# Pooling of an audio layer: eleven of each sixteen pairs multiplied on GpSimd and five on VectorE, sums two products behind

## The reference, cut to what matters

```python
k = 8                                   # x: (128, 64, 750), padded to 752 steps = 94 windows
xp = x.reshape(B, F, nw, k).transpose(0, 2, 3, 1)
scores = einsum('bwkf,of->bwko', xp, w) + b
weights = softmax(scores, axis=2)       # over the 8 steps of a window
pooled = sum(xp * weights, axis=2)      # (128, 94, 64)
```

## Time and profile before

| what | value |
|---|---|
| median of 3 runs | 1019.79 us (1017.86 to 1020.41) |
| the profiled execution, its own time | 1019.19 us |
| its span, first to last instruction | 1017.5 us |
| first spread matmul of the pooling to its last sum | 34.5 to 141.8 us |
| mean granted TensorE clock | 0.944 |

### The profile page before, as it was taken

How to read it: one execution, slowest core, us unless ns; L and a number is a source line. 1 busy time by engine, 2 the same in 40 slices (tenths; PEclk the granted TensorE clock), 3 DMA queues, 4 the chain that set the end, 5 groups by cost and what they waited for, 6 DMA issues and landing times. The chain is left out here.

```text
span 1017.5 us, 37672 instructions
## 1 busy us (share of the span) xinstructions
PE 898.6 (88%) x15018; PEld 577.8 (57%) x15018; DVE 763.6 (75%) x1287; ACT 423.6 (42%) x710; POOL 488.2 (48%) x551
## 2 busy tenths in 40 slices
PE   3677668998937999999999999999999999799995
PEld 2233245555525666666666666666666666446663
DVE  4588863887983888888788888888888888747773
ACT  2333423112713444444444444444444444257774
POOL 3355631110007666666666666666666666212220
PEclk9777877998977999999999999999999999979998
DMA  8765000324102111111111111111111111001111
GB/s 300 263 223 202 1 0 1 55 54 115 31 0 64 50 49 50 52 52 52 48 45 48 50 52 52 52 49 46 48 49 50 52 52 53 2 3 29 29 29 32
DMA packets 64446, 63.25 MB, mean 62 GB/s; under 512 B 37081, under 2 KB 55068, under 8 KB 64412
## 3 DMA queue, kind: packets, MB, share of 16 engines
q1 hardware_dynamic: 63884, 61.25, 20.4%
q10 hardware_dynamic: 528, 1.54, 0.4%
HBM read 52.93 MB, written 6.75 MB: 59 GB/s over the span
## 5 line engine op out<-in xcount | busy, mean ns | idle before, releaser
L1163 ACT ACTIVATE sq<-ps_dot 128x752 f32<-128x752 f32 x192 | 153.1, 798 | 302.6 <-PE ps_dot L1042 302.6
L1042 PE MATMUL ps_dot<-q_st,k_blk 32*64 32x94 f32 x6144 | 169.4, 247 | 3.1 <-POOL k_blk L1002 3.1
L1042 PEld LDWEIGHTS ps_dot<-q_st,k_blk 32*64 32x64 f32 x6144 | 134.4, 133 | 64.6 <-issue 50.0
L1002 POOL TENSOR_TENSOR k_blk<-k_turn,hmask 128x384 f32<-128x384 f32 x64 | 65.3, 1020 | 177.8 <-ACT k_turn L1151 177.8
L1210 DVE TENSOR_REDUCE sums<-prob 128x94 f32<-128x564 f32 x128 | 148.0, 1201 | 2.0 <-ACT prob L1156 2.0
L1006 POOL TENSOR_TENSOR k_mix<-k_cm,cols 128x768 f32<-128x768 f32 x64 | 119.8, 1872 | 0.0
L988 POOL TENSOR_TENSOR v_blk<-v_rep,vmask 128x384 f32<-128x384 f32 x128 | 106.6, 854 | 6.8 <-PE ps_m L1074 6.8
L1091 PEld LDWEIGHTS ps_a<-q_st,k_mix 64*64 64x64 f32 x3072 | 77.1, 132 | 56.4 <-issue 48.2
L1091 PE MATMUL ps_a<-q_st,k_mix 64*64 64x94 f32 x3072 | 101.0, 250 | 0.8 <-DVE prob L1198 0.8
L1156 ACT ACTIVATE prob<-prob,cols 128x564 f32<-128x564 f32 x128 | 91.1, 758 | 20.4 <-DVE prob L1198 20.4
L1181 DVE TENSOR_REDUCE row_max<-ps_a 128x94 f32<-128x564 f32 x128 | 89.3, 741 | 12.4 <-PE ps_a L1110 12.4
(11 more groups left out here) (225 smaller groups left out, 1389.7 us busy)
## 6 DMA issues: line engine op xcount, KB each, us to landing
v_rep<-v_rows SPq DMA_DIRECT2D x256, 96.0 KB
x_g<-in_x_dram SPq DMA_DIRECT2D x15, 1500.0 KB, 6.7
v_rows<-tok SPq DMA_DIRECT2D x32, 96.0 KB
q_st<-q_cm SPq DMA_DIRECT2D x64, 47.0 KB
out_dram<-rows SPq DMA_DIRECT2D x16, 188.0 KB
x_g<-in_x_dram ACTq DMA_DIRECT2D x1, 1500.0 KB, 7.4
top_rows<-tok SPq DMA_DIRECT2D x16, 32.0 KB
top<-top_rows SPq DMA_DIRECT2D x1, 512.0 KB, 3.4
```

The source lines that it names most:

```text
L1002: return pool.tensor_tensor(k_blk[:, a, :, kind], view.unsqueeze(2).broadcast_to([128, NTAU, 4, 8]), k["hmask4"][:].unsqueeze(1).unsqueeze ...
L1042: mm = pe.matmul(ps_dot[64 * hg:64 * hg + 64, (a + g) % 2, b, col:col + N], k_blk[rows, a, 2 * (2 * g + t2) + mi].rearrange("p k h m -> p ...
L1163: act.activation(sq[:, :, :, 2 * g:2 * g + 2, :].rearrange("p mi b t n -> p b mi (t n)"), ps_dot[:, (a + g) % 2, :, 0:4 * N].rearrange("p ...
```

## The change

GpSimd gets eleven pairs of each group (`SENT`: 1, 2, 4, 5, 7, 8, 10, 11, 13, 14, 15), VectorE five (`OWN`: 0, 3, 6, 9, 12). `w_odd` becomes `w_sent`, and the semaphores `even_*` and `odd_*` become `own_*` and `sent_*`. A sent pair may now lie in either place of `ps_spread`, so TensorE waits for whoever reads the pair two before. `sent(g, a, m)` sums GpSimd's product number m; in a group VectorE calls it up to the product that is two behind, so the last four of a group (7 to 10) are summed in the next group, behind its first own product. ScalarE takes the next scores behind its seventh copy instead of its fifth, GpSimd its two parts of the split behind its eighth and ninth product, and VectorE the two halves of the softmax behind its fourth and fifth own pair.

```diff
+    OWN = tuple(range(0, GP - 1, 3))
+    SENT = tuple(n for n in range(GP) if n not in OWN)
...
+    def buffer_of(a, m):
+        return (a * len(SENT) + m) % 2
...
-                        for products in (s["even_done"], s["odd_done"]):
-
-                            sp.wait_ge(products, (2 * n + a - 2) * (GP // 2) + 2 * q + 2)
+                        sp.wait_ge(s["own_done"], (2 * n + a - 2) * len(OWN) + own_before(4 * q + 4))
+                        sp.wait_ge(s["sent_done"], (2 * n + a - 2) * len(SENT) + sent_before(4 * q + 4))
...
-                    pe.wait_ge(s["odd_out" if n % 2 else "even_done"], g * HP + n // 2)
+                    last = (n - 2) % GP
+                    freed, before, per = ("own_done", own_before, len(OWN)) if last in OWN else ("sent_out", sent_before, len(SENT))
+                    if n >= 2:
+                        pe.wait_ge(s[freed], g * per + before(n - 1))
+                    elif not (isinstance(g, int) and g == 0):
+                        pe.wait_ge(s[freed], (g - 1) * per + before(last + 1))
...
-                        for part in {4: (0, 1), 5: (2,), 6: (3,)}.get(n, ()):
+                        for part in {6: (0, 1), 7: (2,), 8: (3,)}.get(m, ()):
                             softmax(g + 1, 1 - a, part)
...
+                    pool.wait_ge(s["sent_out"], g * len(SENT) + m + 1)
+                    if not (isinstance(g, int) and g == 0 and m < 2):
+                        pool.wait_ge(s["sent_pooled"], g * len(SENT) + m - 1)
+                    pool.tensor_tensor(prod[:, 1, at, :], x_g[:, a, n, :], w_sent[:, at, :], ALU.mult).then_inc(s["sent_done"], 1)
...
+                def sent_up_to(end):
+                    nonlocal pooled_up_to
+                    for m in range(pooled_up_to, end):
+                        if m >= 0:
+                            sent(g, a, m)
+                        elif not (isinstance(g, int) and g == 0):
+                            sent(g - 1, 1 - a, m + len(SENT))
+                    pooled_up_to = max(pooled_up_to, end)
+
+                pooled_up_to = sent_before(OWN[-1]) - 1 - len(SENT)
+                for m, n in enumerate(OWN):
+                    dve.wait_ge(s["spread_done"], g * GP + n + 1)
+                    dve.tensor_tensor(halves(prod[:, 0, m % 2, :]), halves(x_g[:, a, n, :]), ps_spread[:, 2 * (n % 2):2 * (n % 2) + 2, 0:HALF],
+                                      ALU.mult).then_inc(s["own_done"], 1)
+                    sent_up_to(sent_before(n) - 1)
+                    dve.wait_ge(s["own_done"], g * len(OWN) + m + 1)
+                    pooled(g, n, 0, prod[:, 0, m % 2, :])
+                    if has_next and m in (3, 4):
+                        softmax(g + 1, m - 3)
+                if not has_next:
+                    sent_up_to(len(SENT))
```

More of the change, by code:

```diff
@@ L301, in pool_windows, with own_before, sent_before @@
     sem = nc.semaphore
-    HP = GP // 2
+    OWN = tuple(range(0, GP - 1, 3))
+    SENT = tuple(n for n in range(GP) if n not in OWN)
+    def own_before(n):
+        return sum(m < n for m in OWN)
+    def sent_before(n):
+        return sum(m < n for m in SENT)
     with ExitStack() as ctx:
         names = ("lo_zero scores_done scores_out maxima shifted exps sums_done inv_done weights_done hi_done rest_done "
-                 "mid_done mid_moved lo_done spread_done even_done odd_out odd_done odd_pooled")
+                 "mid_done mid_moved lo_done spread_done own_done sent_out sent_done sent_pooled")
         s = {n: ctx.enter_context(sem("p_" + n)) for n in names.split()}
@@ L312, in pool_windows @@
         parts = ctx.enter_context(nc.sbuf_tensor("parts", [128, 2, 2, HALF], BF16))
-        w_odd = ctx.enter_context(nc.sbuf_tensor("w_odd", [128, 2, TP], F32))
+        w_sent = ctx.enter_context(nc.sbuf_tensor("w_sent", [128, 2, TP], F32))
         prod = ctx.enter_context(nc.sbuf_tensor("prod", [128, 2, 2, TP], F32))
@@ L406, in group @@
             def group(g, a, twin, has_next):
[L407 to L411, removed]
+                for m, n in enumerate(SENT):
+                    act.wait_ge(s["spread_done"], g * GP + n + 1)
+                    if not (isinstance(g, int) and g == 0 and m < 2):
+                        act.wait_ge(s["sent_done"], g * len(SENT) + m - 1)
+                    at = buffer_of(a, m)
+                    act.activation(halves(w_sent[:, at, :]), ps_spread[:, 2 * (n % 2):2 * (n % 2) + 2, 0:HALF], ACT.Copy).then_inc(s["sent_out"], 1)
                     if has_next:
-                        for part in {4: (0, 1), 5: (2,), 6: (3,)}.get(n, ()):
+                        for part in {6: (0, 1), 7: (2,), 8: (3,)}.get(m, ()):
                             softmax(g + 1, 1 - a, part)
@@ L423, in group @@
             def group(g, a, twin, has_next):
[L424 to L429, removed]
+                for m, n in enumerate(SENT):
+                    at = buffer_of(a, m)
+                    pool.wait_ge(s["sent_out"], g * len(SENT) + m + 1)
+                    if not (isinstance(g, int) and g == 0 and m < 2):
+                        pool.wait_ge(s["sent_pooled"], g * len(SENT) + m - 1)
+                    pool.tensor_tensor(prod[:, 1, at, :], x_g[:, a, n, :], w_sent[:, at, :], ALU.mult).then_inc(s["sent_done"], 1)
+                    if has_next and m == 7:
                         parted(pool, g + 1, 1 - a, "rest")
-                    if has_next and n == 6:
+                    if has_next and m == 8:
                         parted(pool, g + 1, 1 - a, "lo")
@@ L460, in pooled, with sent @@
                 return dve.tensor_reduce(tokens[:, at, 0:N], view.rearrange("p (w k) -> p w k", k=WIN), AX.X, ALU.add)
-            def odd(g, n):
-                dve.wait_ge(s["odd_done"], g * HP + n + 1)
-                pooled(g, 2 * n + 1, 1, prod[:, 1, n % 2, :]).then_inc(s["odd_pooled"], 1)
+            def sent(g, a, m):
+                dve.wait_ge(s["sent_done"], g * len(SENT) + m + 1)
+                pooled(g, SENT[m], 1, prod[:, 1, buffer_of(a, m), :]).then_inc(s["sent_pooled"], 1)
             def group(g, a, twin, has_next):
[L467 to L477, removed]
+                def sent_up_to(end):
[18 more added lines that the diff above has]
+                    sent_up_to(len(SENT))
             softmax(0, 0)
```

## The result

The changed kernel took 1033.54 us in the median of five runs (1033.31 in the shortest), the kernel before 1019.71 beside it: the ratio is 1.0141, with a 95% interval of 1.0126 to 1.0156. That is 13.8 us slower, where the prediction's sum gave 9.5.

A forecast was written before the change was run, and what follows sets the result against it. It took a chain through the engines' queues to end each scored group, and VectorE's pace to bound the last. Three groups at 2.38 us (7.1) plus 2.4 gave 9.5 us: 1028.7, expected median 1029, range 1025.5 to 1034 us.

The forecast's parts named there:

- chain of a scored group: From next scores through softmax and split weights to TensorE's next group: 2.38 us longer in each of three groups, 7.1 us.
- rival B: TensorE's slow clock lasts two more pairs in scored groups: 6.5 us in all, 1035.5 us; full size, shared with C, 0.14.
- small waits: Last group, between GpSimd's thirteen products in a row, because VectorE's four instructions take about as long as GpSimd's two: 0.3 us.
- Scores go out later, +1.54: ScalarE sends scores behind its seventh copy: T (a group's first spread matmul) + 17.80 instead of T + 16.26.
- One more instruction between the softmax halves, +0.84: VectorE, between subtraction and sum of exponentials: product and three sums instead of product and two, 0.84 us per scored group.
- The rest of the chain, 0: First part, rest part, one GpSimd product, low part, TensorE: same instructions in the same order, nothing added.
- GpSimd's stop: After the low part GpSimd waits some 3.5 us for VectorE's late sum at three boundaries; scored groups have room for it.
- The last group, +2.4: GpSimd has 13 products in a row after its stop, so the last group takes 27.2 us instead of 24.8.
- product times on GpSimd still at 1.78: Sign in the changed profile that the forecast is right: GpSimd products take no longer beside VectorE.
- C: Last x_g load of four pairs comes late: at 8 us, 1 us late in two groups, 1031 us; full size, shared with B, 0.14.
- D: VectorE bounds everywhere, so four groups would each gain 2.5 us: 1009 us; chance 0.04.
- E: Nothing to measure: scored groups lose 1 us each through unseen slack, the last group nothing: +3, 1022 us; chance 0.04.

The follow-up runs named there:

- split alone: Against the kernel before: GpSimd eleven pairs, VectorE five, hand-overs as in the changed kernel, but sums one product behind, all inside their group; ratio 1.0153.
- four buffers: The changed kernel with four buffers instead of two for GpSimd's products; 1027.12 us, ratio 1.0076 to the kernel before.
- extra matmuls behind each spread: The changed kernel with unread TensorE score matmuls in the last group, after every spread and fourteen times after the last; 1032.43 us.
- maxima in PSUM: The changed kernel with the softmax's maxima in PSUM instead of SBUF; 1033.72 us in the one execution that can be compared.
- early softmax half: The changed kernel with VectorE taking the second half of the next softmax two sums earlier; 1032.18 us in the one execution that can be compared.
- late sums alone: The kernel before, still split eight and eight with its old hand-overs, only the sums following two products behind; 1020.08 us, ratio 1.0010.
- mended eleven and five: The changed kernel's split with four product buffers, softmax's small results in PSUM, earlier second softmax half, GpSimd's two parts in a row; 1016.17 us, ratio 0.9971.
- matmuls in the gaps: The changed kernel with unread TensorE matmuls in the last group only where TensorE had stood still; last group 27.64 us against 28.91.
- six and ten: Built on the changed kernel: VectorE six pairs, GpSimd ten, five product buffers, softmax's small results in PSUM, earlier hand-overs; 1010.41 us, ratio 0.9912 to the kernel before.

## Why the prediction was too low

The direction and the place were right, the size was not: the sum gave 9.5 us of 13.8. Two steps of it failed. The chain of a scored group left out that the subtraction would take 1.37 us instead of 0.54 (its time was carried over unchanged, in rival B too, where maximum and subtraction count 1.1 us), and the last group's small waits were put at 0.3 us and measured 1.8.

- *Scores go out later, +1.54.* Right: T + 17.90 against T + 17.80 forecast.
- *One more instruction between the softmax halves, +0.84.* Right in the row: product and three sums. Taking two of them off the chain gave 1.0 to 1.6 us in three groups, net of the 3.5 us that it newly cost, which agrees with 0.84 us for each within half a microsecond in all.
- *The rest of the chain, 0: the step that failed.* The 0 held for what stands behind the weights. But in front, between scores and product, I took over the subtraction at 0.54 us, as the row of before has it. In that trace GpSimd stood still beside it each time. The later hand-over put it beside a GpSimd product that had some 0.96 us still to run, and it took 1.37 us: 0.83 us in each of three groups, **2.5 us**, the term that is missing from the sum. I had looked for this contention only on GpSimd's side ("product times on GpSimd still at 1.78"), where there was none.
- *GpSimd's stop.* Right: 3.63, 3.63 and 3.48 us behind the low parts. With it gone the last group was 4.5 us shorter (the clock's share included). That the scored groups don't pay it is shown by the split alone, which had no stop and groups no shorter; in the run with four buffers up to 1.2 us of the second group's gain may be due to it.
- *The last group, +2.4.* Mis-sized: +4.1. The term at fault is the "some 0.3 us of small waits" between the thirteen products: it measured 0.87 + 0.72 + 0.23 = 1.8 us, **1.5 us** more. I gave TensorE's clock no part in it, because GpSimd seemed the bound. But GpSimd waited for a sum, which stood behind a VectorE product, which waited for a spread at the low clock; taking the low clock away brought these waits to 0.4 us and the group down by 1.3. The remaining 0.2 us is in durations slightly above those forecast.
- *The rivals.* B had the clock in the scored groups, where it did little (0.78 against 0.81; pair 10's spread began 0.24 us later in the second group). Its row of before was misread in one point: the granted clock had fallen at 84.28, inside the pause that ended at 86.24, and not behind it. C was not seen in the changed kernel; three other profiles had it in their third group (0.25 us with the extra matmuls behind each spread, 0.89 with the maxima in PSUM, 1.09 with the early softmax half). D and E are out. And the chain that the prediction calls one of five engines' queues runs through four: ScalarE, VectorE, GpSimd and TensorE.

The sum with what was measured: 7.1 + 2.5 + 2.4 + 1.5 = 13.5 us, against 13.8 and 13.2 in the stretch of the two profiles.

## What to carry to other kernels

Moving work from the busiest engine to an idle one pays only if the chain that ends a stage gets no longer: count the instructions that stand in each queue between its links, and price them as they will run beside their new neighbours, not as they ran before. In these runs a VectorE instruction with two SBUF inputs that began beside a running GpSimd product ended only behind it, so its price was what was left of that product, not a share of its own time; a small operand in PSUM took this away. A sum that is put off past a stage's start needs buffers for all products that are made in the meantime, or the producer stands still (3.5 us behind the low part with two buffers, none there with four).

## What the runs showed of the hardware

A VectorE tensor_tensor of 64x376 float32 with both inputs in SBUF took 1.35 to 1.40 us beside a GpSimd product and 0.54 us without one; with one input in PSUM it took 0.54 us beside the product too. Reductions with one input (0.54 us) and products with one input in PSUM (0.92 to 0.94) were not stretched, and GpSimd's product kept its 1.76 to 1.79 us. The Trainium skill (GPSIMD Engine Reference, Specifications) says that GpSimd shares its SBUF interfaces with VectorE and contends with instructions that have two SBUF inputs; these traces agree.

The traces also show what sets the price. In all eighteen stretched instructions (of five profiles) VectorE ended 0.40 us behind the end of the GpSimd product beside it. What that product had left when they began (0.95 to 1.00 us) and their own time (1.35 to 1.40 us) go up and down together. So this is a wait for the product's end, and not a slowdown by a factor. With the late sums alone, three such multiplications began when the product had 0.10 us left, and they took 0.54 us:

```profile
54.79 1.77 POOL L445 TENSOR_TENSOR prod<-x_g,w_sent 128x752 f32<-128x752 f32 x1 [2.82 <-DVE tokens L477]
56.46 0.54 DVE L473 TENSOR_TENSOR soft<-soft,stat 64x376 f32<-64x376 f32 x1
```

By these rows my estimate is: the rest of the product's time, less some 0.14 us (0.97 left at 86.62, 0.83 lost). Not shown is what an instruction pays that begins at other moments of the product, nor who waits where VectorE's instruction is the first to begin: in every case here GpSimd's was.

TensorE can stay at 1.2 GHz while it works without a pause. In the profile of the version with the maxima in PSUM, the next stage ran at a granted clock of 0.50 from 153.7 to 205 us, and TensorE was busy for the whole 37 us from 158 to 195; in that of the changed kernel the same stage reached 1.00 some 4 us after it began (the granted clock is the third number from the right, first of the version with PSUM, then of the changed kernel):

```profile
166.00:170.00 4.00, 4.00 (x20) 3.34 (x19) 1.11 (x2) 0.56 (x2) 0.00 (x0) 0.50 0.00 0
```

```profile
165.00:169.00 4.00, 4.00 (x31) 3.18 (x30) 1.66 (x3) 1.58 (x4) 0.00 (x0) 1.00 0.01 2
```

The work is the same, matmuls of 384 and of 2 columns in turn. By their times it did not happen in any execution of the kernel before, of the sums alone, of the four buffers or of the mended eleven and five. It did in two of ten of the changed kernel, two of four of the split alone, three of four each with the maxima in PSUM, with the early softmax half and with the matmuls in the gaps, and six of ten with six and ten. TensorE had stood still for 7.0 us ahead of the stage in the changed kernel and 4.3 before, but 6.7 us in the mended eleven and five, where the stage came to the fast level in ten executions of ten, and 5.2 us with six and ten; and extra matmuls up to the end of the pooling kept it out in two versions (eight executions), not in the third. So what decides it stays open.
